# A two-layer gated cross-attention and mixture-of-experts kernel: layer 1's routing ranks computed in two parts

## The reference

```python
x = x + tanh(g_xattn[0]) * L0_xattn(layernorm(x), ctx, ...)
x = x + tanh(g_ffn[0])   * L0_ffn(layernorm(x), ...)     # shared expert + top 1 of 8 experts
x = x + tanh(g_xattn[1]) * L1_xattn(layernorm(x), ctx, ...)   # attention, then a two-layer MLP
x = x + tanh(g_ffn[1])   * L1_ffn(layernorm(x), ...)

def L1_ffn(x, Wg, bg, W1, b1, W2, b2, gamma, beta):       # E = 8 experts, top 2
    logits = x @ Wg + bg
    vals, idx = top_k(logits, 2);  w = softmax(vals)
    h  = relu(einsum('bsd,edf->bsef', x, W1) + b1)
    eo = einsum('bsef,efd->bsed', h, W2) + b2
    y  = sum(take(eo, idx) * w) + x
    return gamma * (y - mean(y)) * rsqrt(var(y) + eps) + beta
```

## Time and profile before

| what | us |
| --- | --- |
| times shown, three executions | 1473.31, 1478.64 (median), 1493.58 |
| the profiled execution, its time | 1473.32 |
| its span, first to last instruction | 1471.2 |
| layer 1's attention, last product of its steps ends | 1214.5 |
| expert block of layer 1, first fetch issued | 1274.4 |

### The profile page before, as it was taken

The page is one execution under the profiler, slowest core; times in us unless marked ns, Lnnn a source line. Parts: engine busy times, 40 slices in busy tenths (PEclk is TensorE's granted clock), DMA queues, the critical chain, the costliest instruction groups (busy, mean ns, idle before and its releaser), DMA issues. The chain is left out here.

```text
span 1471.2 us, 31923 instructions
## 1 busy us (share of the span) xinstructions
PE 1343.4 (91%) x13180; PEld 710.2 (48%) x13180; DVE 594.9 (40%) x1259; ACT 981.7 (67%) x1178; POOL 175.2 (12%) x188
## 2 busy tenths in 40 slices
PE   7799999999999997899967999999999996399994
PEld 4433333333333654799932334333333335399983
DVE  7412143152332354333370212652562575544435
ACT  4499999999998233232257995996996990155532
POOL 2000000000000330333300000000000000166540
PEclk9899999999999999899988999999999997599998
DMA  7671010100000813211249110110110215012214
GB/s 208 158 129 28 20 27 20 27 20 24 22 23 22 305 57 126 78 51 47 77 114 193 37 27 15 35 28 16 31 31 25 73 49 168 18 62 76 70 58 172
DMA packets 66267, 101.87 MB, mean 69 GB/s; under 512 B 10218, under 2 KB 48366, under 8 KB 65224
## 3 DMA queue, kind: packets, MB, share of 16 engines
q1 hardware_dynamic: 60168, 83.52, 20.8%
q0 software_dynamic: 5952, 16.26, 3.4%
HBM read 69.04 MB, written 26.21 MB: 65 GB/s over the span
## 5 line engine op out<-in xcount | busy, mean ns | idle before, releaser
L1260 ACT ACTIVATE arena<-ps 128x1024 f32<-128x1024 f32 x556 | 562.5, 1285 | 52.3 <-PE ps L1012 52.3
L1012 PE MATMUL ps<-arena 99*32 99x512 bf16 x6656 | 467.8, 384 | 16.3 <-PEq L860 10.5
L1012 PEld LDWEIGHTS ps<-arena 99*32 99x32 bf16 x6656 | 149.3, 95 | 416.1 <-issue 166.8
L1260 ACT ACTIVATE wqkv<-ps 128x1024 f32<-128x1024 f32 x276 | 303.3, 1285 | 20.6 <-PE ps L1012 20.6
L1028 PE MATMUL ps<-arena 128*32 128x512 f32 x2224 | 289.2, 593 | 0.8 <-ACT arena L1260 0.8
L1342 DVE COPY work<-ps 128x512 f32<-128x512 f32 x30 | 20.7, 692 | 345.0 <-PE ps L1028 345.0
L1825 PEld LDWEIGHTS ps<-work,arena 128*128 128x128 f32 x1184 | 146.2, 197 | 6.5 <-DVE work L1922 3.5
L1825 PE MATMUL ps<-work,arena 128*128 128x128 f32 x1184 | 147.4, 281 | 2.1 <-DVE work L1922 2.1
L1028 PE MATMUL ps<-wqkv,arena 128*32 128x512 f32 x1104 | 144.0, 593 | 0.0
L2026 POOL DMA_INDIRECT work<-xn_img,fetch x62 | 60.4, 975 | 600.2 <-POOLq L992 582.8
L1837 PE MATMUL ps<-arena,work 128*128 x496 | 117.5, 380 | 0.0
(11 more groups left out here) (218 smaller groups left out, 1199.7 us busy)
## 6 DMA issues: line engine op xcount, KB each, us to landing
arena<-in_ew SPq DMA_DIRECT2D x16, 512.0 KB, 5.4
arena<-q_img SPq DMA_DIRECT2D x32, 192.0 KB
arena<-y_tok SPq DMA_DIRECT2D x12, 512.0 KB, 6.4
arena<-k_img SPq DMA_DIRECT2D x8, 624.0 KB, 14.5
q_img<-work SPq DMA_DIRECT2D x18, 256.0 KB, 2.6
k_img<-work SPq DMA_DIRECT2D x21, 208.0 KB, 2.8
arena<-q_img SPq DMA_DIRECT2D x32, 128.0 KB
arena<-in_rg SPq DMA_DIRECT2D x8, 512.0 KB, 7.5
```

The costliest lines, as they stand in the source:

```text
L1012: last = nc.tensor.matmul(ps[i * VW:(i + 1) * VW, buf + j, :], k2[0:ROWS + SHIFT, h, at:at + VW], q2[0:ROWS + SHIFT, h, :], start=True, st ...
L1260: nc.scalar.activation(probs[(b * STEPS + u) % RING], ps[:, buf:buf + 2, :], ACT.Exp, scale=SCALE).then_inc(s_exp, 1)
```

## The change

In layer 1, the entries of blocks 0 to 2 (12 of 16 columns, `FT` = 12) are counted and given their rank while block 3's attention runs; those of block 3 follow behind it, and take the ranks above all of them within each expert. The order of an expert's rows in its tiles becomes another: within the first three blocks by partition and then by column.

- `logits(b - 1)` for all 8 experts and `route(b - 1)` now stand between groups 1 and 2, in blocks 1 to 3; in block 3 `sum_first` follows them (a running sum of the one-hots over the 24 entries of a partition), then group 2.
- PE's `count_first` stands behind step 49 of 52 in block 3: two products with 8 columns each, of the 24 entries' sums, into bank 6.
- DVE's `rank_first` stands behind block 3's additions of `b2` and ahead of `own_tail`: the first entries' slots within their expert, and their `in_row`.
- Behind `route(3)` PE has `count_last` (two products with 8 columns) for `counts`, and DVE `rank_last` for the 32 operations. The start of each expert (`start_e`) comes from one comparison matrix (`earlier`), made in `sum_first`, and is picked by the one-hots for all entries.
- `in_row` of the last block's 8 entries is made in two operations right behind `token_in_tile`, ahead of `past`. `lists` takes the first 24 entries, then the last 8.
- The one-hots of a block, in both layers, are one `tensor_tensor` for each choice (32 elements a partition) in place of four `tensor_scalar`; `s_mx` is gone, and ACT's exponential waits for `s_oh`.
- `in_row[1]` and the new buffers lie over `ctxT`, where the router's rows and their products lay.

```diff
+                    def count_first():
+                        pe.wait_ge(s_fs, 1)
+                        pe.wait_ge(s_u, NB * NG - 1)
+                        nc.tensor.matmul(ps[:, 6, 0:E], below[:, :], first_sum, start=True, stop=True,
+                                         skip_group_check=True)
+                        nc.tensor.matmul(ps[:, 6, E:2 * E], ones[:, :], first_sum, start=True, stop=True,
+                                         skip_group_check=True).then_inc(s_fc, 1)
...
                                 tail(b, w)
                                 if l == 0:
                                     route(b, w)
+                                elif b == NB - 1 and w == NG * NC - 3:
+                                    count_first()
...
+                    def count_last():
+                        pe.wait_ge(s_ls, 1)
+                        nc.tensor.matmul(ps[:, 5, 0:E], below[:, :], last_sum, start=True, stop=True,
+                                         skip_group_check=True)
+                        nc.tensor.matmul(ps[:, 5, E:2 * E], ones[:, :], last_sum, start=True, stop=True,
+                                         skip_group_check=True).then_inc(s_cnt, 1)
...
-                            if i % (T // PIECES) == 0:
-                                pe.wait_ge(s_row, i // (T // PIECES) + 1)
+                        rows = range(T) if l == 0 else [k * NT + t for ts in (range(FT), range(FT, NT)) for k in range(2)
+                                                        for t in ts]
+                        for n, i in enumerate(rows):
+                            if l == 0 and n % (T // PIECES) == 0:
+                                pe.wait_ge(s_row, n // (T // PIECES) + 1)
+                            elif l == 1 and n in (0, 2 * FT):
+                                pe.wait_ge(s_row, 1 if n == 0 else 2)
                             last = nc.tensor.matmul(ps[:, 6, 0:2 * (NTL + 1)], in_row[l][:, i, :],
-                                                    token_in_tile[l][:, i, :], start=(i == 0), stop=(i == T - 1))
+                                                    token_in_tile[l][:, i, :], start=(n == 0), stop=(n == T - 1))
                         last.then_inc(s_list, 1)
...
                         for k in range(L.top):
-                            for t in ts:
-                                last = nc.vector.tensor_scalar(oh[:, k * NT + t, :], iota8[:, :], ixf[:, t, k:k + 1],
-                                                               None, ALU.is_equal)
-                                if k == 0 and t == ts[0]:
-                                    last.then_inc(s_mx, 1)
+                            last = nc.vector.tensor_tensor(oh[:, k * NT + b * TB:k * NT + (b + 1) * TB, :],
+                                                           iota8[:, :].unsqueeze(1).broadcast_to([P, TB, E]),
+                                                           ixf[:, rows, k].unsqueeze(2).broadcast_to([P, TB, E]),
+                                                           ALU.is_equal)
                         last.then_inc(s_oh, 1)
...
+                    def prefix(bufs, n):
+                        i, step_ = 0, 1
+                        while step_ < n:
+                            nc.vector.tensor_copy(bufs[1 - i][:, 0:step_, :], bufs[i][:, 0:step_, :])
+                            nc.vector.tensor_tensor(bufs[1 - i][:, step_:n, :], bufs[i][:, step_:n, :],
+                                                    bufs[i][:, 0:n - step_, :], ALU.add)
+                            dve.drain()
+                            i, step_ = 1 - i, 2 * step_
+                        return bufs[i], bufs[1 - i]
+                    def sum_first():
+                        dve.drain()
+                        for k in range(2):
+                            nc.vector.tensor_copy(scan_first[0][:, k * FT:(k + 1) * FT, :],
+                                                  oh[:, k * NT:k * NT + FT, :])
+                        nc.vector.tensor_tensor(earlier, iota8[:, :].unsqueeze(2).broadcast_to([P, E, E]),
+                                                iota8[:, :].unsqueeze(1).broadcast_to([P, E, E]), ALU.is_gt)
+                        dve.drain()
+                        prefix(scan_first, 2 * FT)
+                        dve.drain().then_inc(s_fs, 1)
+                    def split_ranks(which):
+                        nc.vector.tensor_scalar(which(slot), which(slotf), -1.0, None, ALU.add)
+                        dve.drain()
+                        nc.vector.tensor_scalar(which(rank), which(slot), P - 1, None, ALU.bitwise_and)
+                        dve.drain()
+                        nc.vector.tensor_copy(which(rankf), which(rank))
+                        dve.drain()
+                    def tiles_before(which):
+                        nc.vector.scalar_tensor_tensor(out=which(startf), in0=which(slotf), scalar=-1.0,
+                                                       in1=which(rankf), op0=ALU.add, op1=ALU.subtract)
+                    def rows_of_tiles(ts):
+                        for k in range(2):
+                            js = slice(k * NT + ts.start, k * NT + ts.stop)
+                            n = ts.stop - ts.start
+                            last = nc.vector.tensor_tensor(in_row[1][:, js, :],
+                                                           iota_row[:, :].unsqueeze(1).broadcast_to([P, n, P]),
+                                                           rankf[:, js].unsqueeze(2).broadcast_to([P, n, P]),
+                                                           ALU.is_equal)
+                        last.then_inc(s_row, 1)
+                    def rank_first():
+                        dve.wait_ge(s_fc, 1)
+                        incl, other = first_incl, first_other
+                        nc.vector.tensor_copy(first_cnt.rearrange("p a e -> p (a e)"), ps[:, 6, 0:2 * E])
+                        dve.drain()
+                        nc.vector.tensor_tensor(other, incl, first_cnt[:, 0:1, :].broadcast_to([P, 2 * FT, E]), ALU.add)
+                        dve.drain()
+                        for k in range(2):
+                            nc.vector.tensor_tensor(incl[:, k * FT:(k + 1) * FT, :], other[:, k * FT:(k + 1) * FT, :],
+                                                    oh[:, k * NT:k * NT + FT, :], ALU.mult)
+                        dve.drain()
+                        for k in range(2):
+                            nc.vector.tensor_reduce(slotf[:, k * NT:k * NT + FT], incl[:, k * FT:(k + 1) * FT, :],
+                                                    AX.X, ALU.add)
+                        dve.drain()
+                        split_ranks(first_rows)
+                        tiles_before(first_rows)
+                        rows_of_tiles(slice(0, FT))
+                    def rank_last():
+                        for k in range(2):
+                            last = nc.vector.tensor_reduce(scan_last[1][:, k, :],
+                                                           oh[:, k * NT + FT:(k + 1) * NT, :]
+                                                           .rearrange("p t e -> p e t"), AX.X, ALU.add)
+                        dve.drain()
+                        nc.vector.tensor_tensor(last_sum, scan_last[1][:, 0, :], scan_last[1][:, 1, :], ALU.add
+                                                ).then_inc(s_ls, 1)
+                        for k in range(2):
+                            nc.vector.tensor_copy(scan_last[0][:, k * TB:(k + 1) * TB, :],
+                                                  oh[:, k * NT + FT:(k + 1) * NT, :])
+                        dve.drain()
+                        incl, other = prefix(scan_last, 2 * TB)
+                        dve.wait_ge(s_cnt, 1)
+                        nc.vector.scalar_tensor_tensor(out=padi[:, 0, :], in0=ps[:, 5, E:2 * E], scalar=float(P - 1),
+                                                       in1=first_cnt[:, 1, :], op0=ALU.add, op1=ALU.add)
+                        nc.vector.tensor_tensor(last_before, ps[:, 5, 0:E], first_cnt[:, 1, :], ALU.add)
+                        dve.drain()
+                        nc.vector.tensor_scalar(padi[:, 1, :], padi[:, 0, :], 7, 7, ALU.logical_shift_right,
+                                                ALU.logical_shift_left)
+                        nc.vector.tensor_tensor(other, incl, last_before.unsqueeze(1).broadcast_to([P, 2 * TB, E]),
+                                                ALU.add)
+                        dve.drain()
+                        nc.vector.tensor_copy(padc[:, 0, :], padi[:, 1, :])
+                        for k in range(2):
+                            nc.vector.tensor_tensor(incl[:, k * TB:(k + 1) * TB, :], other[:, k * TB:(k + 1) * TB, :],
+                                                    oh[:, k * NT + FT:(k + 1) * NT, :], ALU.mult)
+                        dve.drain()
```

(72 more changed lines are left out.)

81 lines of the change are left out of this document (53 added, 28 removed).

## The result

The changed kernel takes 1465.03 us (median of four executions, 1462.52 to 1468.57); the kernel before, on the same chip, 1478.3 (median of four, 1473.31 to 1493.58). The ratio of the two is 0.9938, 95% interval 0.9918 to 0.9958: about 9 us less, with an interval from 6 to 12. The medians lie 13.3 us apart. Four executions on each side don't fix the size of the gain; I read it from the stages. The profiled execution took 1468.57, with a span of 1466.8 against 1471.2, only 4.4 us less.

What follows compares the result with a forecast made beforehand. DVE's serial chain between attention and experts was taken as the bound, every microsecond ahead of `places` coming off the end. 4.85 + 4.0 - 0.45 = 8.4 us off a median of 1475.98 gave 1467.6 us, range 1460.5 to 1478.5.

Steps and rivals of the forecast that it cites:

- E: Stage from `places` to the end of the span; forecast unchanged.
- Part 1: First 24 entries' counts and ranks in the shadow of block 3's attention; `last_group` 0.45 us later, bounds 0 and 1.5.
- Part 2: Last block's one-hots, weights and ranks: 0.35 us saved before the ranks, `rank_last` 5.9 for 10.39; `in_tile` 4.85 sooner.
- C: Stage from the last one-hots to `in_tile`; forecast 4.85 us shorter.
- Part 3: Lists, `in_tile` to `places`: 6.0 us for 10.00, so 4.0 saved, bounds 3.6 and 4.4.
- Operations, not elements: Rival, 20%: DVE's price goes by the number of operations, so the gain is 4.9 us, total 1471.1.
- DVE late at `last_group`: Rival, 10%: late counts or dearer drained work start `last_group` 3 to 6 us late; gain 2.4 to 5.4, about 1472.
- Longer stores: Rival, 5%: new row order lengthens the experts' indirect stores; at 1.0 us more each, 1484.8 us, slower than before.
- The clock: PE's clock rate from the lists on: taken as 0, possibly 3.2 us sooner or 1.5 later; early-clock rival 10%, 1464.4.
- B: Stage from `last_group` to the last one-hots; forecast unchanged.
- A: Stage from block 3's group 1 to `last_group`; forecast 0.45 us longer.
- D: Stage from `in_tile` to `places`; forecast 4.0 us shorter.

Runs made afterwards that it cites:

- experiment 7: Changed kernel with `count_first` one attention step sooner; A 46.36 us against 46.71.
- experiment 8: Changed kernel with `count_first` six attention steps sooner, ahead of what it waits for; A 52.91 us.
- experiment 5: Kernel before with the merged one-hots alone, ACT's exponential on `s_oh`; C 10.93 us, 1.23 less.
- Experiments 4 and 3: 4: kernel before, `in_row` pieces moved ahead of `past`, D 9.11 us. 3: changed kernel, first 24 entries' `in_row` made behind `token_in_tile`, D 9.42.
- experiment 6: Changed kernel with ten more drained DVE operations between `rank_last` and `in_tile`, of 8 or 256 elements; C 9.41 and 11.98 us, times 1471.36 and 1469.87.
- experiment 9: Changed kernel with `count_first` one step sooner, weights in the expert block, semaphores for drains in `rank_last` and last norm; 0.9919 of before, 1462.49 us.
- experiment 1: Changed kernel and kernel before run again, no edit; ratio 0.9924, medians 1462.98 against 1473.24 us.

## Why the prediction was right

- **The bound.** Right. What was taken out ahead of `places` came off the end: group 1 to `places` fell by 8.19 us, and E by another 0.53.
- **The DVE price.** Right: 0.07 us an operation, 0.17 a drain, 1.04 ns an element gave `sum_first` 3.5 (measured 3.1 from its first copy to group 2, so some 12% too much), `rank_first` 5.94 (5.88) and `rank_last` 5.9 (5.72).
- **Part 1.** Right. Counts were to reach DVE 40.8 us behind group 1 and did so at 40.83. `last_group` was 0.37 late for 0.45, and experiment 7 shows that `rank_first` is the cause. The cover that I priced at "each us late a us at the end" costs more: experiment 8 paid 6.55 in the attention for 3.87 of idle time, 4.65 of it still at `places`. The step that missed this is the sentence on `count_first`'s wait, which left the clock out. One number is wrong by the prediction's own times: group 2 of block 3 was to be delayed not by 13 us but from 1192.10 to 1200.0, by 7.9; counted from group 1 it came 7.8 later (31.64 for 23.83).
- **Part 2.** Right in its mechanism, small in its size: 0.50 saved by the earlier weights for 0.35 forecast, 4.66 by the ranks for 4.5. In the kernel before it was the counts, not ACT's exponential, that were late in the end (2.02 us idle, experiment 5), so how C divides between one-hots and ranks depends on which comes first; their sum doesn't. No wait for `count_last`, as taken.
- **Part 3.** Right: 6.02 for 6.0. Experiments 4 and 3 divide it into 0.9 of order and 3.1 to 3.4 of rows made early.
- **Operations, not elements.** Fell (experiment 6). **DVE late at `last_group`**: DVE had 2.14 us of idle time, the 2.1 forecast. **Longer stores**: the last store loops take 3.16 to 3.18 us after, 3.17 before, and one tile still takes 3.73 (POOL timeline, after):

```profile
1409.29 0.99 POOL L2205 DMA_INDIRECT y_tok<-work,dest  x1 [1.40 <-DVE work L2125]
...
1413.02 0.99 POOL L2205 DMA_INDIRECT y_tok<-work,dest  x1 [1.47 <-DVE work L2125]
...
1427.16 0.97 POOL L2205 DMA_INDIRECT y_tok<-work,dest  x1 [2.19 <-DMA y_tok<-work,dest]
```

- **The clock.** A term of 0 with a spread of about 3 us was the right size for one stage and too small for the whole: over thirteen profiles B scattered from 33.64 to 36.14, E from 198.0 to 200.5 (196.5 in experiment 9, which edits it), and the way to group 1 by 5.6 us. For B the clock can be read: the four shortest, 33.64 to 34.55, had a granted clock of 0.80 or 0.81 in it, the other nine, 35.54 to 36.14, 0.71 to 0.76.
- **The total.** 1467.6 forecast, 1465.03 measured; 8.4 us lie in the interval 6 to 12 of the ratio, and just inside the 8.0 to 14.4 of experiment 1. The step that I can't call confirmed is the base: the kernel before had a median of 1478.3 beside the result and of 1473.24 over 13 executions in experiment 1, not the 1475.98 that I took from four. That the total came within 2.6 us is thus partly luck; the stages, A, C and D within 0.4 us of their forecast in sum, are not.

## What to carry to other kernels

Work that waits behind a long stage only for its last part can be split, and the first part put where the engine idles; the gain is the covered work less what the split adds, so price both (here 9.9 us of cover less 1.2 that the rest of the change costs on balance, with 2.1 us of room to spare). Cut two profiles at points of the same engine's timeline and compare stage by stage: the stages set by DVE's chain repeated within 0.01 us here, while the totals scattered by several us. On a dependent chain of small DVE operations, widths, drains and waits each have a price that can be read from a few rows, and the sum for the 29 operations of `rank_last` came out within 4%.

## What the hardware did that I had not expected

- A pause of PE of 1.90 to 1.99 us in the attention was followed by 3.4 us at 1.2 GHz in three of thirteen executions, one of 1.93 by none; a stall of 3.87 us cost 6.55 in its stage and 4.65 at `places`. This wait ahead of PE was dearer than its length.
- A semaphore from the last operation of a group is cheaper than a drain for the next small one: 0.20 against 0.24 us start to start.
- With no wait and no drain between them, DVE operations start some 0.08 us before the one in front has ended: `in_row`'s two operations of 1536 elements, 1.75 us each, took 3.42 us together.
- Behind the semaphore of PE's counts DVE went on 0.46 us after PE's last product in the kernel before and 0.11 after it with the one-hots merged; no run here says why.
